# A row choice by repeated take-out of the eight largest, in the attention loop of a four-layer kernel

## The chip, the cores and the metric

One Trainium2 chip, one core. The time is the device time of one execution in microseconds (us). The engines are named as the profile names them: PE is the matrix engine (PEld is its loading of weights), DVE the vector engine, ACT the scalar engine, POOL the GpSimd engine, SP the one that issues DMAs.

## The reference

Four layers, each an attention part and a feed-forward part, on x (2 batches, 256 rows, 512 wide) and a context ctx (2 batches, 512 rows, 512 wide). Two parts matter here.

```python
# layer 2, attention: 32 query heads, 8 groups of keys and values, 128 wide
q, k = rmsnorm(q, q_norm_w), rmsnorm(repeat(k, 4), k_norm_w)
scores = einsum('bhqd,bhkd->bhqk', q, k) * scale + attention_mask      # 512 keys
out = einsum('bhqk,bhkd->bhqd', softmax(scores), v)
return out.transpose(...).reshape(B, Q, 32 * 128) @ o_proj_w.T

# layer 3, attention part: a choice among ctx's rows, for every batch and column
k = 154                                              # from 0.6 * 256, made even
_, topk_idx = top_k(moveaxis(ctx, 1, 2), k)          # largest 154 of 512, for each of 512 columns
mask = zeros(2, 512, 256).at[..., topk_idx].set(1.0) # indices of 256 and above drop out
crucial, subcrucial = mask * x, (1 - mask) * x       # then a small gate for each of the two
```

So before layer 3 can start, each of 2 x 512 columns of ctx needs the 154 largest of its 512 values marked, of which the first 256 places are used. This depends on ctx alone, so it can be worked out at any time before.

## The kernel before

ctx lies transposed in SBUF as `k.ctxT`, 128 partitions by 4 column blocks by 2 batches x 512 values. A "row tile" (`row_tile`, line 2280) is one block and batch: 128 partitions x 512 f32, eight of them (r = 0 to 7).

**The choice before.** A search by bits for each partition's 154th largest value. One round is four `bisection_count` calls (line 2320), each comparing two row tiles with the candidate bits and adding up the hits (L2324, 128x512), and one `bisection_update` of five tiny operations (L2374 to L2381, 128x8 and 128x16). Thirty-one rounds are spread over DVE's program: a start (eight counts at L2289, then L2297 to L2310) and the first counts in the layer-1 attention (one count call each at its units 40, 45, 50 and 55, an update behind the last), four counts in the layer-1 feed-forward part, four more and an update at the start of the layer-2 attention, and then two rounds in each of its steps. When the bits are found, `choose_piece` (line 2340) marks the chosen places, with the first ones first among equals, in five pieces for two row tiles: a count (L2347), equality (L2351) and the number left (L2352), a running sum (L2355), a comparison (L2358), an addition (L2362). Row tiles 0 and 1 are treated in units 4 to 7 of step 14, the other six in step 15.

**The layer-2 attention** (`layer2_attention`, line 1542) is 16 steps, one per group of heads and batch, numbered 0 to 15. Step 0 stands by itself, steps 1 to 14 are pairs in a hardware loop on PE, ACT and POOL; on DVE the loop holds steps 1 to 12, and 13 and 14 are written out. Step 15 is `run_final`. Every step has 8 units u (a head and 128 queries). In a unit, PE turns the probabilities (`turn_probs`, L1826), multiplies the scores of unit u + 2 (`scores`), and does a piece of other work: the projections of keys, values and queries of the next step (u = 0 to 4), the output projection of the step before (u = 5 to 7, `project_out`), the mix of probabilities and values (`mix`). ACT takes the exponentials (L1999) and casts the turned probabilities to their high part (L2007). DVE takes the low part (L2134, `probsT_low`), masks scores and takes their maximum (L2122, `maximum`), adds the output into x (L2140, `add_out`), and at the end of the unit runs two counts of the search. The order on each engine is the order of the code; engines meet by semaphores. There are two PSUM banks for scores (S) and two for turned probabilities (T), so PE's unit u + 2 needs DVE's maximum and ACT's exponential of unit u.

**Step 15** divides by the sum of exponentials ahead of the turn: DVE takes the reciprocal (L2181), scales the identity with it (L2183, `divided`), and PE multiplies by this diagonal (L1845, `turn_divided`). The mixed heads are split by ACT and DVE (`head_high`, `head_low`) and projected head by head (`project_final`, L1856). Two units of `project_out` for step 14 stand in it as well; they need POOL's scaling of step 14's heads (L1697, L1701, L1703), which in turn needs step 13's `add_out` of both halves. POOL also makes the low part of the weights in the loop (L1666, L1670, L1676; 2.4 to 4.6 us each).

## Time and profile before

| | us |
|---|---|
| median of 3 runs | 869.71 (868.5 to 871.69) |
| profiled execution | 867.53, with a span of 865.7 and 1.83 around it |
| busy in the span: PE / DVE / ACT / POOL | 779.5 / 716.7 / 517.8 / 416.6 |
| layer-2 attention, steps 1 to 14 | 273.7 to about 738.6 |
| layer-2 attention, step 15 | about 739 to 786 |

The times of single instructions come from one profiled execution. A row's microseconds are busy time; two instructions of an engine can overlap a little, so the distance from start to start says more about what an instruction takes. Idle time in brackets stands ahead of the row that ended it, with what released it. In a step a PE that is busy all the time sets the pace; a wait of PE is named with the engine that released it.

### The profile page before, as it was taken

To read this page: it belongs to the slowest core of one execution; us is meant where nothing else is said; L and a number is where in the kernel's file an instruction comes from. 1 tells how busy PE (TensorE), PEld (TensorE's weight loads), DVE (VectorE), ACT (ScalarE), POOL (GpSimd) and SP (SyncE) were. 2 spreads that over 40 slices of the span, in tenths; PEclk is the share of its full clock that TensorE was granted. 3 is DMA by queue.
4 is the path that set the end of the run, shared out by engine and by line. 5 is a ranking of instruction groups with operands and counts; after the bars stand their busy time and mean duration, and the time that the engine had idled before them with its cause. 6 is when DMAs were issued, how large, how long until landed. Compare 5 with 4: busy or idle time off the path is not lost. (4 is left out here: it accounts for less than half of the span.)

```text
span 865.7 us, 16485 instructions
## 1 busy us (share of the span) xinstructions
PE 779.5 (90%) x5172; PEld 633.8 (73%) x5178; DVE 716.7 (83%) x1751; ACT 517.8 (60%) x1407; POOL 416.6 (48%) x372
## 2 busy tenths in 40 slices
PE   1976899958987999999999999999999999689878
PEld 0474676534776898998898898898898898576356
DVE  7878998968787887887887887887887897894985
ACT  6865798836456756756656657657557557331521
POOL 3237078705236745745746746745744844501110
PEclk9999999979999999999999999999999999899989
DMA  8254246453202201201300300310220320003001
GB/s 308 92 170 149 75 149 217 157 167 108 68 32 59 88 26 52 94 24 45 101 24 26 119 25 22 109 39 14 86 71 0 97 73 0 25 1 119 1 1 48
DMA packets 38298, 66.65 MB, mean 77 GB/s; under 512 B 5553, under 2 KB 18417, under 8 KB 38130
## 3 DMA queue, kind: packets, MB, share of 16 engines
q1 hardware_dynamic: 38258, 66.15, 23.2%
q8 instruction: 21, 0.34, 0.2%
q14 instruction: 19, 0.16, 0.1%
HBM read 60.81 MB, written 5.34 MB: 76 GB/s over the span
## 5 line engine op out<-in xcount | busy, mean ns | idle before, releaser
L1999 ACT ACTIVATE layer_attention_probs<-xnT,stats 128x512 f32<-128x512 f32 x128 | 93.9, 734 | 134.1 <-DVE stats L2122 134.1
L2324 DVE TENSOR_SCALAR_CACHE_REDUCE xn<-ctxT,candidate 128x512 bf16<-128x512 f32 x240 | 168.7, 741 | 0.0
L1747 PE MATMUL bank<-layer_attention_keysT,layer_attention_queriesT 128*128 128x512 f32 x384 | 122.4, 427 | 5.0 <-DVE layer_attention_queriesT L2115 5.0
L2134 DVE TENSOR_TENSOR layer_attention_probsT<-bank,layer_attention_probsT 128x512 fp32r<-128x512 f32 x128 | 88.1, 688 | 42.2 <-ACT layer_attention_probsT L2007 40.8
L2007 ACT CAST layer_attention_probsT<-bank 128x512 fp32r<-128x512 f32 x128 | 74.9, 585 | 54.0 <-PE bank L1826 47.7
L1747 PEld LDWEIGHTS bank<-layer_attention_probsT,layer_attention_values 128*128 128x128 f32 x768 | 98.5, 188 | 11.7 <-DVE layer_attention_probsT L2134 6.5
L1747 PE MATMUL bank<-layer_attention_probsT,layer_attention_values 128*128 128x256 f32 x768 | 101.3, 281 | 3.4 <-DVE layer_attention_probsT L2134 3.0
L1747 PE MATMUL bank<-layer_attention_l_wq,layer_attention_xnT 128*128 128x512 f32 x384 | 93.7, 392 | 0.0
L1747 PEld LDWEIGHTS bank<-layer_attention_l_wkv,layer_context_parts 128*128 128x128 f32 x720 | 88.4, 188 | 2.8
L1747 PE MATMUL bank<-layer_attention_l_wkv,layer_context_parts 128*128 128x256 f32 x720 | 90.3, 278 | 0.0
L1747 PE MATMUL bank<-layer_attention_wo,layer_attention_headsT 128*128 128x512 f32 x336 | 88.8, 406 | 0.0
L2122 DVE CUSTOM_DVE_ANT_0 xnT<-bank,layer_attention_mask 128x512 f32<-128x512 f32 x128 | 87.0, 680 | 0.6 <-PE bank L1747 0.5
L1697 POOL TENSOR_TENSOR layer_attention_mixed<-layer_attention_mixed,xnT 128x512 f32<-128x512 f32 x30 | 49.1, 1636 | 68.9 <-DMA xnT<-inverse_sums 64.1
L1747 PEld LDWEIGHTS bank<-layer_attention_l_wq,layer_attention_xnT 128*128 128x128 f32 x384 | 70.9, 188 | 15.1 <-issue 0.2
L1826 PE MATMUL bank<-ident,layer_attention_probs 128*128 128x128 f32 x480 | 71.8, 272 | 0.4 <-ACT layer_attention_probs L1999 0.4
L1747 PEld LDWEIGHTS bank<-layer_attention_keysT,layer_attention_queriesT 128*128 128x128 f32 x384 | 63.4, 192 | 11.6 <-issue 5.8
L1747 PEld LDWEIGHTS bank<-layer_attention_wo,layer_attention_headsT 128*128 128x128 f32 x336 | 60.0, 189 | 11.5
L1826 PEld LDWEIGHTS bank<-ident,layer_attention_probs 128*128 128x128 f32 x480 | 57.5, 140 | 10.5 <-issue 0.6
L270 POOL TENSOR_TENSOR rstd<-varep,minus_half 128x1 f32<-128x1 f32 x24 | 14.9, 631 | 95.3 <-DVE varep L226 66.7
L1682 POOL TENSOR_SCALAR layer_attention_ssq<-layer_attention_ssq 128x4 f32<-128x4 f32 x48 | 9.3, 193 | 90.5 <-ACT layer_attention_squares L1958 90.5
L1958 ACT ACTIVATE layer_attention_squares<-bank 128x128 f32<-128x128 f32 x192 | 52.0, 299 | 0.0
L1687 POOL TENSOR_TENSOR xn<-xn,layer_attention_ssq 128x512 f32<-128x512 f32 x47 | 48.9, 1040 | 3.7
(332 smaller groups left out, 1716.1 us busy)
## 6 DMA issues: line engine op xcount, KB each, us to landing
layer_attention_l_raw_qo<-in_wqT SPq DMA_DIRECT2D x9, 1024.0 KB, 5.1
xnT<-inverse_sums SPq DMA_DIRECT2D x15, 512.0 KB, 3.7
layer_attention_l_raw_qo<-in_woT SPq DMA_DIRECT2D x7, 1024.0 KB, 6.9
tw_raw<-in_w_gateT SPq DMA_DIRECT2D x8, 688.0 KB, 5.5
tw_raw<-in_w_upT SPq DMA_DIRECT2D x8, 688.0 KB, 4.3
tw_raw<-in_w_downT SPq DMA_DIRECT2D x6, 768.0 KB, 4.6
layer_attention_l_raw_kv<-in_wkvT SPq DMA_DIRECT2D x9, 512.0 KB, 4.9
ternary<-tw_rounded SPq DMA_DIRECT2D x8, 344.0 KB, 2.5
```

The costliest lines, as they stand in the source:

```text
L270: g.tensor_tensor(k.rstd[:, t:t + 1], k.varep[:, t:t + 1], k.minus_half[:, 0:1], ALU.pow).then_inc(k.tile_rstd, 1)
L1682: own(g.tensor_scalar(ssq[:, c, :], ssq[:, c, :], 1.0 / HD, EPS, ALU.mult, ALU.add))
L1687: g.tensor_tensor(r, r, ssq[:, c, :].unsqueeze(2).broadcast_to([P, REP, HD]), ALU.mult)\
L1697: g.tensor_tensor(now, now, factors, ALU.mult).then_inc(S_["mix_scaled"], 1)
L1747: last = pe.matmul(out, stationary[f][a], moving[f][b], start=f == 0 and x == 0, stop=f == count - 1 and x == 2)
L1826: last = pe.transpose(T[u % 2][:, c * P:(c + 1) * P], probs[:, u % 3, c * P:(c + 1) * P], k.ident[:, :])
L1958: return a.activation(squares[:, h, :], source, ACT.Square, accum_out=ssq[:, c, h:h + 1])
L1999: a.activation(probs[:, u % 3, :], masked[:, u % 2, :], ACT.Exp, bias=negmax[:, u:u + 1], scale=-1.0, accum_out=sums[:, u:u + 1]).then_inc ...
L2007: a.copy(probsT[:, 0, p % 2, :, u % 2 * P:(u % 2 + 1) * P], T[u % 2][:, :].rearrange("p (c q) -> p c q", c=CPB)).then_inc(S_["probsT_high" ...
L2122: v.tensor_tensor_reduce(masked[:, u % 2, :], S[u % 2][:, :], mask[:, u % TPB, :], -1.0, 3.4e38, ALU.add, ALU.min, negmax[:, u:u + 1]).the ...
L2134: v.tensor_tensor(probsT[:, 1, p % 2, :, columns], T[u % 2][:, :].rearrange("p (c q) -> p c q", c=CPB), probsT[:, 0, p % 2, :, columns], A ...
L2324: own(k.nc.vector.tensor_scalar((k.flags if flags is None else flags)[:, r % 2], row_tile(k.ctxT, r), k.candidate[:, r:r + 1].bitcast(F32) ...
```

## The change

The search by bits goes, with its buffers, its flags and all its counts and updates. In its place each row tile's eight largest values are found (`largest`, the vector engine's max) and then taken out, that is, overwritten in place by the lowest f32 (`take_out`, match_replace), 20 times. 154 is 19 times 8 and 2, so ahead of the last take-out six of the eight values are set to the lowest f32 (`leave_rest`). What was overwritten is then turned into ones (`flag`, 128x256, the half that is used). A pass is 16 operations over 128x512 f32: one pass in step 0 (two operations a unit), 18 in steps 1 to 12 (three a unit), the last in step 13, the eight flags in step 14 (one a unit). Nothing of it is left in step 15, in the layer-1 parts, or ahead of step 0.

In step 15, DVE's division of unit u + 1 and ACT's exponential of unit u + 2 are issued in unit u. DVE's `probsT_low` follows the maximum in the same unit, and the two `add_out` come at u = 5 and 6. On PE `project_out` moves from u = 5, 6 to u = 4, 5, and three of the four `project_final` move ahead of the last mix.

```diff
+def largest(k, own, r):
+    own(k.nc.vector.max(k.top[:, r, :], row_tile(k.ctxT, r)))
+def take_out(k, own, r):
+    own(k.nc.vector.match_replace(row_tile(k.ctxT, r), k.top[:, r, :], row_tile(k.ctxT, r), GONE))
+def leave_rest(k, own):
+    own(k.nc.vector.memset(k.top[:, :, TOPK % TAKEN:TAKEN], GONE))
+def flag(k, own, r):
+    row = row_tile(k.ctxT, r)[:, 0:SEQ]
+    own(k.nc.vector.tensor_scalar(row, row, GONE, None, ALU.is_equal))
...
+    OPS = 2 * CTILES
+    ROUND = [(op, r) for half in range(2) for op in (largest, take_out) for r in range(half * CTILES // 2, (half + 1) * CTILES // 2)]
+    PER_BODY = 3
...
+                def search(step, u, own):
+                    if step[0] is not None:
+                        ops = (ROUND * PER_BODY)[(step[1] - 1) * PER_BODY * CTILES:step[1] * PER_BODY * CTILES]
+                    elif step[1] < STEPS - 2:
+                        ops = ROUND
+                    else:
+                        ops = [(flag, r) for r in range(CTILES)]
+                    now = ops[u * len(ops) // UNITS:(u + 1) * len(ops) // UNITS]
...
-                        if u < chosen_from:
-                            bisection_count(k, own, u % 4)
-                            if u % 4 == 3:
-                                bisection_update(k, own)
...
+                            search(step, u, own)
...
                 def run_final(step):                      # PE
...
+                        if u in (4, 5):
+                            for half in range(2):
+                                project_out(before, u - 4, half, weights=wq)
                         if u in (3, 5, 7):
                             mix(step, u // 2 - 1, final=True)
-                        if u in (5, 6):
-                            for half in range(2):
-                                project_out(before, u - 5, half, weights=wq)
-                    project_final(step, 0)
+                        if u in (6, 7):
+                            project_final(step, u - 6)
+                    project_final(step, 2)
                     mix(step, PAIRS - 1, final=True)
-                    for h in range(1, REP):
-                        project_final(step, h)
+                    project_final(step, 3)
...
                 def run_final(step):                      # DVE
+                    divided(step, 0)
+                    probsT_low(before, UNITS - 1)
+                    maximum(step, 1)
                     for u in range(UNITS):
-                        if u:
-                            probsT_low(step, u - 1)
-                        else:
-                            probsT_low(before, UNITS - 1)
-                        divided(step, u)
                         if u + 1 < UNITS:
-                            maximum(step, u + 1)
+                            divided(step, u + 1)
                         if u in (4, 6):
                             head_low(u // 2 - 2)
-                        if u == 7:
-                            add_out(before, 0)
-                        for r, piece in pieces[u * len(pieces) // UNITS:(u + 1) * len(pieces) // UNITS]:
-                            choose_piece(k, own, r, piece)
-                    probsT_low(step, UNITS - 1)
-                    add_out(before, 1)
+                        if u + 2 < UNITS:
+                            maximum(step, u + 2)
+                        probsT_low(step, u)
+                        if u in (5, 6):
+                            add_out(before, u - 5)
```

DVE in the loop, before, unit 7 of the first step of the pair and what follows it. Here L2324 is a count, L2374 to L2381 the update, L2140 the `add_out`, L2134 `probsT_low`; REGISTER_ALU rows only work out what a wait compares with.

```order
L2324 TENSOR_SCALAR xn,counts<-ctxT,candidate 128x512 x2
L132 REGISTER_ALU
L2374 SCALAR_TENSOR_TENSOR enough<-counts,flip 128x8
L132 REGISTER_ALU
L2376 TENSOR_TENSOR set_bit<-enough,bits 128x8
L132 REGISTER_ALU
L2378 TENSOR_TENSOR found<-found,set_bit 128x8
L2379 TENSOR_SCALAR bits<-bits 128x16
L132 REGISTER_ALU
L2381 TENSOR_TENSOR candidate<-found,bits 128x8
L2138 REGISTER_ALU
L2140 TENSOR_TENSOR x<-bank,x 128x512
```

The same place after the change. L2276 is a take-out, L2125 the `add_out`, L2119 `probsT_low`.

```order
L2123 REGISTER_ALU
L2125 TENSOR_TENSOR x<-bank,x 128x512
L132 REGISTER_ALU
L2276 MATCH_REPLACE ctxT<-top,ctxT 128x512 x3
L2123 REGISTER_ALU
L2125 TENSOR_TENSOR x<-bank,x 128x512
L2119 TENSOR_TENSOR layer_attention_probsT<-bank,layer_attention_probsT 128x4x128
L2103 REGISTER_ALU
```

Two counts and five tiny operations have become three take-outs; in units without an update, two counts have become three operations.

DVE where step 14 ends and step 15 begins, before. L2358 and L2362 are pieces of the choice, L2347 another; L2181 and L2183 the division, L2122 the maximum with its second row.

```order
L2140 TENSOR_TENSOR x<-bank,x 128x512
L2358 SCALAR_TENSOR_TENSOR ctxT<-ctxT,left 128x256 x2
L2362 TENSOR_TENSOR ctxT<-xn,ctxT 128x256 x2
L2140 TENSOR_TENSOR x<-bank,x 128x512
L2134 TENSOR_TENSOR layer_attention_probsT<-bank,layer_attention_probsT 128x4x128
L2181 RECIPROCAL layer_attention_last_inverse<-stats 128x1
L2183 TENSOR_SCALAR layer_attention_diagonal<-ident,layer_attention_last_inverse 128x128
L2122 ISA xnT,stats<-bank,layer_attention_mask 128x512
L2122 ISA stats 128x1
L2347 TENSOR_SCALAR xn,above<-ctxT,found 128x512 x2
L2134 TENSOR_TENSOR layer_attention_probsT<-bank,layer_attention_probsT 128x4x128
```

After the change, from the same `add_out` (L2125) on. L2287 is a flag, L2185 and L2187 the division, L2107 the maximum.

```order
L2125 TENSOR_TENSOR x<-bank,x 128x512
L2287 TENSOR_SCALAR ctxT<-ctxT 128x256
L2125 TENSOR_TENSOR x<-bank,x 128x512
L2185 RECIPROCAL layer_attention_last_inverse<-stats 128x1
L2187 TENSOR_SCALAR layer_attention_diagonal<-ident,layer_attention_last_inverse 128x128
L2119 TENSOR_TENSOR layer_attention_probsT<-bank,layer_attention_probsT 128x4x128
L2107 ISA xnT,stats<-bank,layer_attention_mask 128x512
L2107 ISA stats 128x1
L2185 RECIPROCAL layer_attention_last_inverse<-stats 128x1
L2187 TENSOR_SCALAR layer_attention_diagonal<-ident,layer_attention_last_inverse 128x128
L2107 ISA xnT,stats<-bank,layer_attention_mask 128x512
```

Four operations of the choice (x2 each for L2358 and L2362) are gone from ahead of the first division, one flag is in their place, and the division now stands ahead of `probsT_low` (L2119).

PE at the end of step 15, before. Products with headsT are `project_out`, with probsT and values a mix, L1856 `project_final`, L1845 a turn.

```order
L1747 MATMUL bank<-layer_attention_probsT,layer_attention_values 128x256 x12
L1747 MATMUL bank<-layer_attention_l_wq,layer_attention_headsT 128x512 x12
L1845 MATMUL bank<-layer_attention_diagonal,layer_attention_probs 128x128 x4
L1747 MATMUL bank<-layer_attention_l_wq,layer_attention_headsT 128x512 x12
L1845 MATMUL bank<-layer_attention_diagonal,layer_attention_probs 128x128 x4
L1747 MATMUL bank<-layer_attention_probsT,layer_attention_values 128x256 x12
L1856 MATMUL bank<-layer_attention_l_wq,layer_attention_xnT 128x512 x6
L1747 MATMUL bank<-layer_attention_probsT,layer_attention_values 128x256 x12
L1856 MATMUL bank<-layer_attention_l_wq,layer_attention_xnT 128x512 x18
```

After the change; L1839 is `project_final`, L1828 a turn.

```order
L1730 MATMUL bank<-layer_attention_l_wq,layer_attention_headsT 128x512 x12
L1730 MATMUL bank<-layer_attention_probsT,layer_attention_values 128x256 x12
L1828 MATMUL bank<-layer_attention_diagonal,layer_attention_probs 128x128 x4
L1839 MATMUL bank<-layer_attention_l_wq,layer_attention_xnT 128x512 x6
L1828 MATMUL bank<-layer_attention_diagonal,layer_attention_probs 128x128 x4
L1730 MATMUL bank<-layer_attention_probsT,layer_attention_values 128x256 x12
L1839 MATMUL bank<-layer_attention_l_wq,layer_attention_xnT 128x512 x12
L1730 MATMUL bank<-layer_attention_probsT,layer_attention_values 128x256 x12
L1839 MATMUL bank<-layer_attention_l_wq,layer_attention_xnT 128x512 x6
```

Six products of `project_final` now stand behind the turn of unit 6, twelve behind the mix of unit 7, and six instead of eighteen are left behind the last mix.

## Rows read from the trace of the kernel before

**Rows 1.** stretches (us): length; busy (count) of PE, PEld, DVE, ACT, POOL; clock; DMA
```profile
438.03:470.86 32.83, 32.83 (x216) 29.36 (x215) 26.49 (x76) 21.08 (x64) 16.12 (x16) 1.00 0.05 16
470.86:503.86 33.00, 32.86 (x214) 29.02 (x213) 29.08 (x75) 20.58 (x63) 23.08 (x18) 1.00 0.30 95
602.52:636.88 34.36, 32.85 (x214) 29.01 (x213) 30.46 (x76) 20.58 (x63) 23.14 (x18) 1.00 0.28 92
744.50:780.00 35.50, 28.22 (x164) 24.32 (x165) 31.14 (x83) 11.32 (x26) 5.62 (x5) 0.90 0.00 1
```

**Rows 2.** whom PE waited for, whole span: us, times, longest
```profile
PE bank L1845 <- DVE layer_attention_diagonal L2183: 11.9, 5, 5.2
PE bank L1747 <- DVE layer_attention_probsT L2134: 3.0, 4, 1.5
```

**Rows 3.** instructions in time (start, us, engine): counts in the loop
```profile
440.98 0.74 DVE L2324 TENSOR_SCALAR_CACHE_REDUCE xn<-ctxT,candidate 128x512 bf16<-128x512 f32 x1
441.64 0.74 DVE L2324 TENSOR_SCALAR_CACHE_REDUCE xn<-ctxT,candidate 128x512 bf16<-128x512 f32 x1
...
443.21 0.69 DVE L2140 TENSOR_TENSOR x<-bank,x 128x512 f32<-128x512 f32 x1
```

**Rows 4.** groups by line: busy us, mean ns; first operation of the update
```profile
L2374 DVE SCALAR_TENSOR_TENSOR enough<-counts,flip 128x8 f32<-128x8 f32 x31 | 24.7, 798 | 1.0
```

**Rows 5.** instructions in time, DVE in the router's choice after this layer
```profile
798.40 0.61 DVE L2605 MAX8 tail_best<-tail_expd 128x8 f32<-128x64 f32 x4 [0.48 <-ACT tail_expd L2765]
799.04 0.09 DVE L2608 MATCH_VALUE_LOAD tail_rest<-tail_best,tail_expd 128x8 f32 x1
...
799.25 0.08 DVE L2608 MATCH_VALUE_LOAD tail_rest<-tail_best,tail_expd 128x8 f32 x1
```

**Rows 6.** instructions in time, DVE, a reduction over 512 columns
```profile
86.39 1.89 DVE L1066 TENSOR_REDUCE layer_attention_negmax<-bank 128x1 f32<-128x512 f32 x3
```

**Rows 7.** instructions in time, DVE, POOL and PE, 608 to 611 us
```profile
608.08 1.52 DVE L2381 TENSOR_TENSOR candidate<-found,bits 128x8 int32<-128x8 int32 x1
607.99 1.58 POOL L1697 TENSOR_TENSOR layer_attention_mixed<-layer_attention_mixed,xnT 128x512 f32<-128x512 f32 x1 [0.46 <-DMA xnT<-inverse_sums]
610.85 1.67 PE L1747 MATMUL bank<-layer_attention_probsT,layer_attention_values 128*128 128x256 f32 x12 [1.51 <-DVE layer_attention_probsT L2134]
```

**Rows 8.** instructions in time, PE in the last step
```profile
738.97 0.96 PE L1747 MATMUL bank<-layer_attention_keysT,layer_attention_queriesT 128*128 128x512 f32 x3
745.17 2.04 PE L1845 MATMUL bank<-layer_attention_diagonal,layer_attention_probs 128*128 128x128 f32 x8 [5.24 <-DVE layer_attention_diagonal L2183]
...
749.65 1.05 PE L1845 MATMUL bank<-layer_attention_diagonal,layer_attention_probs 128*128 128x128 f32 x8
...
781.00 4.28 PE L1856 MATMUL bank<-layer_attention_l_wq,layer_attention_xnT 128*128 128x512 f32 x18
```

**Rows 9.** instructions in time, DVE and POOL in the last step
```profile
738.45 4.19 DVE L2358 SCALAR_TENSOR_TENSOR ctxT<-ctxT,left 128x256 f32<-128x256 f32 x2
753.49 1.14 DVE L2183 TENSOR_SCALAR layer_attention_diagonal<-ident,r_attention_last_inverse 128x128 f32<-128x128 f32 x1
736.01 4.60 POOL L1670 TENSOR_TENSOR layer_attention_l_wq<-layer_attention_l_raw_qo,layer_attention_l_wq 128x2048 fp32r<-128x2048 f32 x1 [3.51 <-ACT layer_attention_l_wq L2023]
740.84 1.52 POOL L1697 TENSOR_TENSOR layer_attention_mixed<-layer_attention_mixed,xnT 128x512 f32<-128x512 f32 x1 [0.23 <-DMA xnT<-inverse_sums]
753.28 1.26 POOL L1703 TENSOR_TENSOR layer_attention_headsT<-layer_attention_mixed,layer_attention_headsT 128x512 fp32r<-128x512 f32 x1
```

**Rows 10.** instructions in time, end of the layer-1 attention
```profile
170.20 0.69 ACT L1170 ACTIVATE layer_attention_probs<-bank,layer_attention_negmax 128x512 f32<-128x512 f32 x1 [2.61 <-DVE layer_attention_negmax L1066]
171.03 0.57 PE L964 MATMUL bank<-l_keysT,layer_attention_queriesT 128*128 128x512 f32 x1 [1.84 <-ACT layer_attention_probs L1170]
172.74 1.58 POOL L270 TENSOR_TENSOR rstd<-varep,minus_half 128x1 f32<-128x1 f32 x3
```

**Rows 11.** instructions in time, start of the layer-2 attention
```profile
247.15 0.93 PE L1747 MATMUL bank<-layer_attention_keysT,layer_attention_queriesT 128*128 128x512 f32 x3 [1.49 <-DVE layer_attention_queriesT L2115]
```

More of the change, by code:

```diff
@@ L1097, in latent_low @@
                      .then_inc(S_["latent_low"], 1)
-                k.flags = mixed[:, :].bitcast(BF16).rearrange("p (j c) -> p j c", j=2)
-                for j in range(4):
-                    bisection_start_count(k, own, j)
-                k.flags = k.xn[:, 3, :].bitcast(BF16).rearrange("p (j c) -> p j c", j=2)
                 value_copy(0)
@@ L2240, in _ @@
                 rowsT_low(start, KEYS)
-                for j in range(FRONT_COUNTS, 4):
-                    bisection_count(k, own, j, first_flags(k))
                 rowsT_low(start, 0)
```

156 lines of the change are left out of this document (33 added, 123 removed).

## The prediction

> **What bounds the kernel now.** I read the stretches first, one per step of the layer-2 attention. Steps without and with POOL's low parts take 32.83 and 33.00 us, and PE is busy for 32.83 and 32.86 of them at full clock [rows 1]. So the loop goes at PE's pace; DVE is busy 26.49 and 29.08 us, 27.8 in the mean. One step takes 34.36 us with the same work on PE. The next view, whom PE waited for, has only 3.0 us for `probsT_low` in the whole span, one wait being 1.5, but 11.9 us in five waits for the diagonal L2183 [rows 2]. That diagonal exists only in step 15, and there PE is busy 28.22 of 35.50 us at a clock of 0.90 [rows 1]. The instructions in time then tell who held DVE. Less search work on DVE is therefore worth nothing in most of the loop. The change is worth what it frees in step 15, and in the few places where an update or a count stands in front of something that PE needs.
>
> **The loop, steps 1 to 12.** A step has 16 counts. From start to start a count takes 0.66 to 0.67 us [rows 3], so 10.7 us go. Two updates go with them. The one at 442.31 takes 0.90 us up to `add_out` at 443.21 [rows 3]. But L2374 alone averages 798 ns over 31 updates [rows 4], many times what eight columns need, because it is often held up; I put an update at 1.5, two at 3.05. DVE's other work is then 27.8 − 10.7 − 3.05 = 14.1 us a step.
>
> Added are 24 operations a step, 12 maxima and 12 take-outs over 512 columns. The trace has both kinds only at 64 columns, in the router. Four maxima are busy 0.61 us together, the last for about 0.21, so they start 0.133 us apart; a load of the eight values and its replacement take 0.20 us (799.04 to 799.25) [rows 5]. For the 448 further columns I take the count's rate: it takes 0.67 us for 512, hardly anything being fixed, and three reductions over 512 columns are busy 1.89 us, 0.63 each [rows 6]. At 0.467 us for 448 columns a maximum takes 0.60 and a take-out 0.67. That is 12 x 0.60 + 12 x 0.67 = 15.2 us, and DVE comes to 29.3 of PE's 32.9 us, 89%. The bounds: below, nothing runs faster than the router's pieces, 0.133 and 0.20, which would leave DVE lighter than before at no gain, PE being full; above, a kind could run at half that rate, 0.93 us more than the 64-column price, 1.07 and 1.13. The lot may average (32.9 − 14.1) / 24 = 0.78 us until DVE sets the pace. I take 0.60 and 0.67, since both one-input rows over 512 columns lie there.
>
> PE hides all of that. What can be gained is PE's waits. In step 602.52 to 636.88, L2381 (128x8, two inputs) took 1.52 us beside POOL's L1697 of 1.58, and PE's mix at 610.85 waited 1.51 for the `probsT_low` behind it [rows 7]. The holds that I see fell on operations with two tensor inputs from SBUF, as here, or on the diagonal; the new operations have one, like the count, so I expect nothing of the choice to be held there: −1.5. Steps of 33.00 against 32.86 busy lose 0.14, six or seven times: −0.9. Against it, a unit without an update now has three operations instead of two, 1.9 to 2.0 us for 1.33. The slack for `probsT_low` there is small where another 0.14 us wait is already seen, so a few tenths a step may come back. I take nothing and keep up to 0.5 a step, 6 us, for the range.
>
> **Step 15.** PE goes from 739.75 (738.97 and a last score of step 14, busy 0.96, whose three products leave PE to step 15 after some 0.78) to 785.28 (781.00 + 4.28) [rows 8], 45.5 us. 11.9 are waits for the diagonal. The clock was 0.90 over 35.5 us, that is, its lower level for a fifth of them; a turn takes 2.04 us there and 1.05 at the full one [rows 8]. Half of 7 us would be 3.5, some of it inside waits; I take 3.1. Work is 45.5 − 11.9 − 3.1 = 30.5, 30.1 by the durations at full clock.
>
> The waits that come in their place:
> - The first turn waited 5.24 [rows 8], because L2358 held DVE (two, 4.19 us, from 738.45) with L2362 behind, beside POOL's L1670 (4.60 from 736.01) and L1697 (1.52 from 740.84) [rows 9]. Those pieces go, but POOL's do not. A flag, `add_out` and the division stand there now, and the diagonal took 1.14 us for 128 columns when it met L1703 [rows 9], where a count's rate would give under 0.3; a diagonal that meets L1697 ends only at 742.36. I put the first turn at 742.7, a wait of 2.95.
> - For units 2 and 3, maximum, exponential and division form a chain: two operations over 512 columns at 0.7 to 0.85 each [rows 3, 10] and 0.4 for reciprocal and diagonal, 2.0 to 2.2 us a unit, against a little less of PE's work: 1.2.
> - `project_out` now comes a unit earlier and `project_final` sits behind `add_out` of the same bank: 1.35. The last head's split before the last six products: 1.1.
>
> Together 6.6. The end is at 739.75 + 30.1 + 6.6 = 776.4, so 785.28 − 776.4 = 8.9, with the clock at full level because the longest stop is shorter; I take 9.1 with a small head start from step 14's shorter DVE program. Bounds: no wait at all gives 15; if each wait is only moved (POOL being the holder) 0 to 3.
>
> **The ends of the search elsewhere.** At the end of the layer-1 attention the last count and update stood ahead of the last maximum; ACT waited 2.61 for it and PE 1.84 behind [rows 10]. That goes, but POOL's rstd at 172.74 comes behind its own queue [rows 10] and holds the next normalization, so I take 1.6, between 0.5 and 3.2. At the start of the layer-2 attention four counts and an update go; PE's first scores waited 1.49 for the query rows [rows 11], which come 0.35 to 0.6 earlier: 0.6, at most 1.5. The counts at the very start and in the layer-1 feed-forward part stand where DVE waits for others anyway: nothing.
>
> **Sum.** 9.1 + 1.6 + 0.6 + 0.9 + 1.5 = 13.7. The profiled execution took 867.53, so 853.8. The median of the runs is 869.71, 2.2 above it: 856.0. With step 15's likely 6 to 13 and the small terms, this case alone spans 852 to 860.
>
> **Rivals.**
> - *The new operations set the pace (slower).* If the take-out costs 1.13 us, half rate, a step of DVE is 14.1 + 12 x 1.13 + 12 x 0.60 = 34.9 us, 2.0 above PE; twelve steps 24, plus waits that no longer pair up, 25: 856 + 25 = 881. It decides from a mean of 0.78. If both are slow, a step is 40.5 and the kernel about 950. For it: no 512-column row of either exists. Against it: the 64-column pair takes 0.20 us including a load, so that at half rate it would have only 0.07 fixed. Chance 0.10.
>  The Trainium skill, Vector Engine (DVE) Microarchitecture Reference, section "The match/index hardware and the swap-based sort pattern", describes the replacement as one preparing step and then one steady step over the stream, and the maximum as a chain of seventeen steps. By the first the take-out runs at one element a cycle, as the rival denies; the router's row of 0.20 us agrees, but no row here shows the 512-column case.
> - *The shorter slack gives it back.* 0.5 us a step in 12 steps, 6 us: 862. For it: DVE goes from 85 to 89% and each of 6 light units gets 0.6 us more. Against it: unit 7, the one with the updates and the stops, gets lighter. Chance 0.10.
> - *Step 15 stays held by POOL.* Divisions and flags meet L1697 and L1703 again, and only 3 of the 9 come: 862. For it: [rows 9]. Against it: the division now stands a unit ahead, so one hold is covered. Chance 0.07.
>  The Trainium skill, SBUF — State Buffer, section "SBUF: two separate sides", says that DVE and POOL share a port pair that one instruction holds to its end, wanted by DVE when it reads two inputs from SBUF or runs in a two-port mode. [Rows 7] (1.52 beside 1.58) agree. By it, the one-input maxima and take-outs pass POOL freely and only diagonals and flags are caught, which is this rival, with 3 us for 9.
> - *More than this*, PE without waits in step 15 and the layer-1 stop gone fully: 9 → 14 and 1.6 → 3, 849. Chance 0.08.
> The forecast has 0.65.
>
> 0.5% of the time, 4.35 us, is about what a measurement of this kernel tells from no change. Faster by more means below 865.4. The forecast, the last rival and nearly all of the two at 862 lie there, though their tails do not, and the first rival is slower: 0.82 faster, 0.08 the same, 0.10 slower. The range must leave out no more than a fifth: 850 to 866 leaves out the slow rival and half of the last.
>
> **What the profile of after would show.** MAX8 and the replacement over 128x512 near 0.68 us busy, 0.60 and 0.67 from start to start; a mean over 0.78 refutes the loop's term. PE busy about 32.8 of each step with DVE at 29.3 or so; a step of 33.4 is the second rival. No wait for `probsT_low` of 1.5 us. In step 15, waits for the diagonal of 6 us or less in all, the first of about 3, a clock of 0.95 or more; if the first is still 5, POOL was the holder. At the layer-1 end ACT's wait of 2.61 gone. The prediction is wrong above all if either new operation runs at half rate, since 288 of them stand in the loop.

## The result and the profile after

The changed kernel took 853.93 us in the median (853.17 to 858.18, 4 runs), the kernel before 870.32 (868.5 to 871.69), a ratio of 0.983 (0.981 to 0.985). Forecast were 856.0 and a range of 850 to 866. The profiled execution has a span of 851.5 us against 865.7, which is 14.2 less; the medians lie 16.4 apart.

First the stretches of the changed kernel (called after from here on): two steps of the loop that follow each other, one earlier step that differs, and step 15. Columns as in [rows 1].

```profile
432.60:465.40 32.80, 32.80 (x214) 29.38 (x213) 29.06 (x69) 21.30 (x64) 16.11 (x16) 1.00 0.05 16
465.40:498.20 32.80, 32.80 (x215) 29.39 (x214) 29.24 (x69) 20.77 (x63) 23.13 (x18) 1.00 0.29 96
337.31:370.94 33.63, 33.09 (x214) 29.46 (x213) 28.91 (x69) 20.57 (x63) 19.34 (x18) 1.00 0.28 95
729.50:771.30 41.80, 34.69 (x204) 29.38 (x203) 23.24 (x53) 13.10 (x30) 10.22 (x7) 0.96 0.04 14
```

Where [rows 1] had 32.83 and 33.00 us, the loop's ordinary steps now take 32.80. PE is busy in all of it, and DVE is busy 29.06 and 29.24. One step still takes 33.63, where PE waited 0.54 us for the values' low parts. In step 15 the granted clock is 0.96, and DVE is busy 23.24 of 41.80 us, where it was busy 31.14 of 35.50.

The two new operations, by their line: count, shortest, median and longest duration in ns, first and last start. Then places in time where several stand in a row:

```profile
L2276 DVE MATCH_VALUE_LOAD ctxT<-top,ctxT x160: 70/82/89, 248.4 to 694.8; 128x8 f32 x160
L2276 DVE MATCH_REPLACE8 ctxT<-top,ctxT x160: 670/676/681, 248.5 to 694.9; 128x512 f32<-128x512 f32 x160
```

```profile
L2271 DVE MAX8 top<-ctxT x160: 673/681/693, 242.6 to 680.9; 128x8 f32<-128x512 f32 x160
```

```profile
501.65 0.67 DVE L2276 MATCH_REPLACE8 ctxT<-top,ctxT 128x512 f32<-128x512 f32 x1
...
502.31 0.68 DVE L2276 MATCH_REPLACE8 ctxT<-top,ctxT 128x512 f32<-128x512 f32 x1
...
504.70 1.87 DVE L2271 MAX8 top<-ctxT 128x8 f32<-128x512 f32 x3
```

Both run at one rate: three maxima are busy 1.87 us, so they start 0.60 apart ((1.87 − 0.68) / 2), and two take-outs start 0.66 apart (501.65 to 502.31), load included. Forecast were 0.60 and 0.67. None of the 320 is stretched: the longest took 693 ns, though POOL was at work beside some two thirds of them, and 115 of them began while a POOL operation of over 1.2 us still had 0.15 us or more to go.

Whom PE waited for, of which [rows 2] had 11.9 and 3.0 us:

```profile
PE bank L1828 <- DVE layer_attention_diagonal L2187: 3.6, 3, 2.5
...
PE bank L1839 <- DVE x L2125: 1.3, 1, 1.3
...
PE bank L1839 <- DVE layer_attention_xnT L2192: 0.9, 1, 0.9
```

The wait for `probsT_low` in the loop is gone. In step 15 PE waits 3.6 + 1.3 + 0.9 = 5.8 us, where the forecast had 6.6. The rows in time, to be read against [rows 8, 9], show where the longest of these waits comes from:

```profile
728.21 4.60 POOL L1653 TENSOR_TENSOR layer_attention_l_wq<-layer_attention_l_raw_qo,layer_attention_l_wq 128x2048 fp32r<-128x2048 f32 x1 [3.51 <-ACT layer_attention_l_wq L2007]
732.92 1.51 POOL L1680 TENSOR_TENSOR layer_attention_mixed<-layer_attention_mixed,xnT 128x512 f32<-128x512 f32 x1
```

```profile
730.65 2.31 DVE L2287 TENSOR_SCALAR ctxT<-ctxT 128x256 f32<-128x256 f32 x1
732.89 0.68 DVE L2125 TENSOR_TENSOR x<-bank,x 128x512 f32<-128x512 f32 x1
...
733.67 0.85 DVE L2187 TENSOR_SCALAR layer_attention_diagonal<-ident,r_attention_last_inverse 128x128 f32<-128x128 f32 x1
```

```profile
734.66 2.05 PE L1828 MATMUL bank<-layer_attention_diagonal,layer_attention_probs 128*128 128x128 f32 x8 [2.55 <-DVE layer_attention_diagonal L2187]
```

The flag that now stands where L2358 stood is held for 2.31 us, up to the end of POOL's 4.60 (732.81); six of the eight flags take 0.28 to 0.39. The diagonal behind it takes 0.85 us and ends about when POOL's 1.51 does (734.52 and 734.43). The turn starts 2.55 us late.

**Where the gain sits.** One profiled execution is one sample, and the twelve experiments below share most of the kernel, so each stretch has up to thirteen samples of after's code and one of before's. In this table a stretch runs from an instruction to an instruction: the first reduction L1064 of the layer-1 attention (L1066 in before), the first turn of layer_ffn_x, the first, ninth, 113th and 121st maximum of the layer-2 attention, PE's first product behind it, and the end of DVE's last addition. "Same code" is the mean over all traces of kernels whose code in the stretch is that of after, with their number and the lowest and highest.

| stretch | before | after | same code as after |
|---|---|---|---|
| start to layer-1 attention | 86.4 | 86.2 | 88.0 (13; 85.8 to 91.8) |
| layer-1 attention | 100.7 | 96.3 | 97.2 (11; 96.3 to 97.8) |
| layer-1 feed-forward, start of layer 2 | 57.9 | 56.3 | 57.9 (13; 56.3 to 58.9) |
| step 0 | 30.3 | 31.5 | 30.9 (13; 30.4 to 33.0) |
| steps 1 to 13 | 429.1 | 426.5 | 426.8 (8; 425.4 to 427.5) |
| step 14 | 32.8 | 32.7 | 32.7 (13; 32.7 to 32.7) |
| step 15 | 49.4 | 41.9 | 41.9 (9; 40.7 to 42.4) |
| behind it | 76.6 | 77.6 | 77.8 (13; 75.8 to 79.1) |

Three stretches are shorter than before by more than the same code scatters: the layer-1 attention by 3.4 us, steps 1 to 13 by 2.4, step 15 by 7.5, together 13.3. In the other stretches before lies within the same code's scatter or 0.1 us beside it, although the feed-forward part, the start of layer 2 and step 0 lost counts too; the very start alone spans 6 us. The trace pair's own difference, 14.2, is larger than 13.3 by chance: after's trace is shorter than the same-code mean by 1.6 us in the feed-forward part and by 0.9 in the layer-1 attention, while its step 0 and what lies behind step 15 took 1.2 and 1.0 more than before's.

The 13.3 us are not all of the difference between the medians, which differ by 16.4 here and by 15.6 in a second session. Before was traced once, in an execution 2.8 us below its median, so the runs don't show where the other 2 to 3 us lie.

### The profile page after: what moved, and what is told of

It reads as the page before. It is cut to its first block and busy times, and to the rows that moved or that the text cites. A ratio compares the mean times of both kernels' runs of the same rounds, so it can differ in the third digit from the quotient of the medians.

```text
span 851.5 us, 16269 instructions
## 1 busy us (share of the span) xinstructions
PE 777.6 (91%) x5178; PEld 637.2 (75%) x5178; DVE 681.0 (80%) x1512; ACT 520.2 (61%) x1407; POOL 416.0 (49%) x372
## 5 line engine op out<-in xcount | busy, mean ns | idle before, releaser
L1730 PE MATMUL bank<-layer_attention_keysT,layer_attention_queriesT 128*128 128x512 f32 x384 | 120.6, 422 | 4.2 <-DVE layer_attention_queriesT L2100 4.1
L2119 DVE TENSOR_TENSOR layer_attention_probsT<-bank,layer_attention_probsT 128x512 fp32r<-128x512 f32 x128 | 87.4, 683 | 44.0 <-ACT layer_attention_probsT L1991 43.0
L2276 DVE MATCH_REPLACE8 ctxT<-top,ctxT 128x512 f32<-128x512 f32 x160 | 106.9, 676 | 0.0
L2271 DVE MAX8 top<-ctxT 128x8 f32<-128x512 f32 x160 | 102.4, 681 | 0.0
L1730 PE MATMUL bank<-layer_attention_l_wkv,layer_context_parts 128*128 128x256 f32 x720 | 92.9, 281 | 0.0
L1730 PEld LDWEIGHTS bank<-layer_attention_l_wkv,layer_context_parts 128*128 128x128 f32 x720 | 90.7, 188 | 2.5
L2107 DVE CUSTOM_DVE_ANT_0 xnT<-bank,layer_attention_mask 128x512 f32<-128x512 f32 x128 | 87.1, 680 | 5.3 <-PE bank L1730 5.1
L1064 DVE TENSOR_REDUCE layer_attention_negmax<-bank 128x1 f32<-128x512 f32 x64 | 43.4, 685 | 9.4 <-PE bank L962 8.7
```

The lines of the kernel that those rows point to most:

```text
L1064: v.tensor_reduce(negmax[:, tile(u), head(u):head(u) + 1], S[u % 3][:, :], AX.X, ALU.max, negate=True)\
L1730: last = pe.matmul(out, stationary[f][a], moving[f][b], start=f == 0 and x == 0, stop=f == count - 1 and x == 2)
L2107: v.tensor_tensor_reduce(masked[:, u % 2, :], S[u % 2][:, :], mask[:, u % TPB, :], -1.0, 3.4e38, ALU.add, ALU.min, negmax[:, u:u + 1]).the ...
L2119: v.tensor_tensor(probsT[:, 1, p % 2, :, columns], T[u % 2][:, :].rearrange("p (c q) -> p c q", c=CPB), probsT[:, 0, p % 2, :, columns], A ...
L2271: own(k.nc.vector.max(k.top[:, r, :], row_tile(k.ctxT, r)))
L2276: own(k.nc.vector.match_replace(row_tile(k.ctxT, r), k.top[:, r, :], row_tile(k.ctxT, r), GONE))
```

## The experiments

Each is an edit of the changed kernel, timed beside runs of the kernel before on the same chip. Since the start of the kernel scatters by 6 us with no edit, a median tells differences of some 4 us only; the verdicts on smaller ones rest on the stretch that the edit touches, with the table's same-code scatter as the measure. Each of these stretches was traced once for each kernel.

### The changed kernel again

> The changed kernel once more, as the base for its neighbours on this chip. 853 to 855 us, ratio 0.983 to the kernel before. If the two-microsecond scatter of its tail (a TensorE clock that falls around 811 us in the earlier trace) is chance, the part behind the layer-2 attention may differ by up to 1 us from the earlier trace.

857.04 us (852.69 to 858.89), ratio 0.9825 (0.979 to 0.986). The expected 853 to 855 was missed, but the ratio holds: the median moved 3 us with the session, and that of the kernel before 2. Its trace has 78.1 us behind step 15, which is less than 1 us from after's 77.6, as expected, and a step 15 of 40.7. That step ran at a granted clock of 1.00, where after's ran at 0.96. In the nine traces of step 15's unchanged code there are two at 1.00, with 40.7 and 40.9 us, and seven at 0.96, with 41.9 to 42.4, 42.2 in the mean. The small differences below are therefore also read against the mean at the same clock.

### Step 15 with the old order

```diff
 def run_final(step):                      # DVE; PE and ACT likewise as before
-    divided(step, 0)
-    probsT_low(before, UNITS - 1)
-    maximum(step, 1)
     for u in range(UNITS):
+        probsT_low(step, u - 1) if u else probsT_low(before, UNITS - 1)
-        if u + 1 < UNITS: divided(step, u + 1)
+        divided(step, u)
...
```

> The changed kernel with the old order of step 15 on PE, ACT and DVE; the choice pieces stay gone. It splits the 7.5 us that the traces show for step 15 into the pieces' removal and the new order. My expectation: the pieces carry more than half; without the look-ahead each unit's division waits for its exponential again and the end has three head products after the last split: 3 us given back, 857. Rival A (the order carries it): 860 to 861. Rival B (the pieces carry all): 854.

858.52 us, ratio 0.985 (0.982 to 0.988), and step 15 takes 42.8 us (same code 41.9). By this the order is worth 0.9 us of the 7.5, and 0.6 if only traces at this kernel's clock of 0.96 are compared; the removed pieces are worth the remaining 6.6; they were not put back by themselves. That is rival B but for a microsecond, and my 3 us was too much. PE's waits show what the order does:

```profile
PE bank L1828 <- DVE layer_attention_diagonal L2185: 6.6, 4, 2.7
```

With the old order PE waits 6.6 us for diagonals, 3.0 more than in after, but none for `add_out` or for a head's split (1.3 + 0.9 in after). The new order has 3.0 us less of waits for the diagonal and pays for them with 2.2 us of waits at the end.

### What holds the first turn: flags later, diagonals on ACT, both

```diff
-                        ops = [(flag, r) for r in range(CTILES)]
+                        ops = [(flag, r) for r in range(CTILES - 2)]   # late_flags: one a unit, u = 0 to 5
...
+                        if u in (3, 4):                                # late_flags, step 15
+                            flag(k, own, CTILES - 2 + u - 3)
```

```diff
-                    v.wait_ge(S_["last_inverted"], u + 1)              # act_diag: gone from DVE
-                    v.tensor_scalar(diagonal[:, u % 2, :], k.ident[:, :], last_inverse[:, u:u + 1], None, ALU.mult)
+                    a.wait_ge(S_["last_inverted"], u + 1)              # act_diag: on ACT, u + 1 in unit u
+                    a.activation(diagonal[:, u % 2, :], k.ident[:, :], ACT.Copy, scale=last_inverse[:, u:u + 1])
```

> The last two of the eight flags move from step 14 behind the maxima of units 3 and 4 of step 15. Theory (the flag held by POOL sets the first turn): the first wait for the diagonal falls from 2.55 to about 1.2, since the diagonal itself then waits for POOL's 4.6 us operation that ends near 732.8 and for the next; 852.7 us. Rival (POOL is the holder, whatever stands first): 2.5 us stays, 854.

> ACT instead of DVE scales the identity in step 15; all else as changed. Theory (DVE and POOL hold each other for operations on the identity): the diagonal no longer takes 0.85, 0.82 and 0.45 us in units 0, 2, 3, and the waits of 0.72 and 0.31 us go; the first wait stays near 2.0 because the flag in front of the reciprocal is still held 2.3 us. 852.7 us, 1.2 less. Rival (the waits are the chain of maximum, exponential and division, whoever does the last): 854, no change.

> Both edits together: nothing of DVE's that POOL can hold stands between the last exponential of step 14 and the first turns of step 15. Theory: the first wait falls to 0.3 or less, units 2 and 3 have none, the clock stays at its upper level there: 3.6 us of waits and some 1 us of slow turns go, 850 us. Rival (the turns then wait for the scores' maxima instead, the chain through DVE and ACT): 852.5 us.

| | median us | ratio to before | step 15 us | clock there | PE's waits for the diagonal |
|---|---|---|---|---|---|
| changed kernel, same session | 857.04 | 0.9825 (0.979 to 0.986) | 40.7 (same code 41.9) | 1.00 | 2.7, 0.7, 0.3 |
| flags later | 852.11 | 0.9765 (0.973 to 0.980) | 39.1 | 1.00 | 0.9, 1.0, 0.3 |
| diagonals on ACT | 855.96 | 0.9818 (0.978 to 0.986) | 41.3 | 0.96 | 0.3, 0.4; 2.1 for `probsT_low` |
| both | 854.22 | 0.9789 (0.975 to 0.983) | 38.0 | 1.00 | 0.4, 0.3, 0.4 |

Rows in time of the flags-later kernel around its first turn, PE, DVE and POOL:

```profile
733.58 4.60 POOL L1653 TENSOR_TENSOR layer_attention_l_wq<-layer_attention_l_raw_qo,layer_attention_l_wq 128x2048 fp32r<-128x2048 f32 x1 [3.52 <-ACT layer_attention_l_wq L2007]
...
737.18 1.09 DVE L2187 TENSOR_SCALAR layer_attention_diagonal<-ident,r_attention_last_inverse 128x128 f32<-128x128 f32 x1
...
738.41 1.13 PE L1828 MATMUL bank<-layer_attention_diagonal,layer_attention_probs 128*128 128x128 f32 x8 [0.93 <-DVE layer_attention_diagonal L2187]
...
742.39 1.58 POOL L1680 TENSOR_TENSOR layer_attention_mixed<-layer_attention_mixed,xnT 128x512 f32<-128x512 f32 x1
...
742.99 1.07 DVE L2187 TENSOR_SCALAR layer_attention_diagonal<-ident,r_attention_last_inverse 128x128 f32<-128x128 f32 x1
...
744.21 1.13 PE L1828 MATMUL bank<-layer_attention_diagonal,layer_attention_probs 128*128 128x128 f32 x8 [0.97 <-DVE layer_attention_diagonal L2187]
```

With the flag away the diagonal itself meets the same POOL operation: it ends at 738.2, when POOL's 4.60 us from 733.58 do. Unit 2's takes 1.07 us beside POOL's 1.58. So POOL's operation is what the diagonal waits out both times, and the flag only made it longer. ACT's scaling is not held, as the kernel with both edits shows; the last row is the stretch of its step 15, columns as in [rows 1]:

```profile
731.64 4.62 POOL L1653 TENSOR_TENSOR layer_attention_l_wq<-layer_attention_l_raw_qo,layer_attention_l_wq 128x2048 fp32r<-128x2048 f32 x1 [3.52 <-ACT layer_attention_l_wq L2007]
...
735.35 0.40 ACT L2019 ACTIVATE layer_attention_diagonal<-ident,r_attention_last_inverse 128x128 f32<-128x128 f32 x1
...
735.90 1.13 PE L1828 MATMUL bank<-layer_attention_diagonal,layer_attention_probs 128*128 128x128 f32 x8 [0.38 <-ACT layer_attention_diagonal L2019]
...
740.48 0.40 ACT L2019 ACTIVATE layer_attention_diagonal<-ident,r_attention_last_inverse 128x128 f32<-128x128 f32 x1 [0.23 <-DVE r_attention_last_inverse L2195]
740.48 1.52 POOL L1680 TENSOR_TENSOR layer_attention_mixed<-layer_attention_mixed,xnT 128x512 f32<-128x512 f32 x1
...
741.02 1.13 PE L1828 MATMUL bank<-layer_attention_diagonal,layer_attention_probs 128*128 128x128 f32 x8 [0.31 <-ACT layer_attention_diagonal L2019]
...
732.86:770.87 38.01, 33.38 (x204) 28.20 (x203) 18.36 (x46) 15.91 (x38) 10.33 (x7) 1.00 0.05 15
```

Both of ACT's take 0.40 us with POOL at work beside them, and the first turn waits 0.38. Step 15 is at 38.0 us, 3.9 under the same-code mean and 2.7 under the lowest of the nine. PE's waits for diagonals fell from 3.6 us to 1.1; 3.6 of waits and 1 of slow turns were expected to go. Against the two same-code traces that ran at 1.00 too, with 40.8 us in the mean, the gain is 2.8 us, which is what the waits explain (3.8 and 3.9 us in those two, 1.1 here). The rest of the 3.9 is the clock, and that the edits brought it to 1.00 isn't shown, since the unedited code reached it with a first wait of 2.7 us. Each edit alone brought less: the later flags 2.7 us, 1.7 at the same clock; the diagonals on ACT 0.6, 0.9 at the same clock, since the flag still stood in front and PE's first turn then waited 2.1 us for `probsT_low`. Whether these kernels beat the changed one in the median can't be told, as the intervals overlap.

### The layer-1 calls put back

```diff
+                    if u in (40, 45, 50, 55):                          # l1_last: only 55
+                        own.wait()
+                        for r in range(2 if u < 55 else 4):
+                            largest(k, own, r)
```

> The changed kernel with a stand-in for the last count call and update in the layer-1 attention: four maxima over 512 columns, 2.4 us of DVE against 2.66 before, at unit 55. The prediction counted 1.6 us for this place, because POOL's rstd behind was thought to hold the rows: by it 855.5. By the two traces' starts the place is worth 3.5 us up to the next scores' product and some 1.6 us more at the lower clock: 857.5 to 859.

> As l1_last, with two maxima each at units 40, 45 and 50 as well. By the prediction, which counted the earlier calls at nothing, 855.5; by the traces, where PE stood 1.4 us earlier at the corresponding place ahead of the last call, 1.4 us more than l1_last: 859 to 860.4.

858.19 us, ratio 0.9855 (0.983 to 0.989), and 861.37, 0.987 (0.984 to 0.991). The stretch of the layer-1 attention in four kernels, before, after, last call, all calls:

```profile
86.40:187.10 100.70, 86.14 (x900) 61.25 (x901) 87.80 (x173) 79.03 (x198) 54.60 (x43) 0.96 0.42 139
```

```profile
86.20:182.50 96.30, 83.30 (x900) 60.14 (x901) 80.53 (x143) 78.95 (x198) 54.78 (x43) 0.96 0.44 145
```

```profile
87.60:186.30 98.70, 83.75 (x899) 59.66 (x899) 83.71 (x147) 78.93 (x198) 55.07 (x43) 0.97 0.42 141
```

```profile
89.50:190.30 100.80, 85.18 (x900) 60.89 (x901) 87.08 (x154) 79.14 (x198) 55.04 (x43) 0.94 0.41 138
```

Four calls bring 100.8 us, where before had 100.7; the last call alone brings 98.7 against 97.2. That makes the last call and its update worth 1.5, as the prediction had it, and not the 3.5 and more that I read from the two traces; the three calls ahead of it, counted at nothing, are worth the other 1.9. That the calls together carry the whole 3.4 us is clear of the same code's scatter of 96.3 to 97.8. How they share it is less certain: each share rests on one trace, and 98.7 lies only 1.0 above that scatter.

### The loop without the choice, and with more of it

```diff
-                        ops = (ROUND * PER_BODY)[...]        # no_take
+                        ops = []
...
                     for op, r in now:
                         op(k, own, r)
+                    if step[0] is not None and u in (0, 2, 4, 6):      # loop_28; loop_32: every u
+                        own(v.max(k.spare[:, u % 3, :], mask[:, 0, :]))
```

> Steps 1 to 12 without any maximum or take-out; the other passes stay. Leaves out 18 of the 20 passes of the row choice. Theory (PE sets the loop's pace and hides DVE's 29 of 32.8 us): 0.3 to 1 us less, 853.2. Rival (the tight units still cost a few tenths a step): 3 to 6 us less, 848 to 851.

> One more maximum over 512 columns in units 0, 2, 4 and 6 of steps 1 to 12: 28 operations a step, DVE 29.15 + 4 x 0.61 = 31.6 of PE's 32.8 us. Theory (only the sum against PE's step matters): 0 to 2 us more, 855. Rival (a single unit that is too full passes its delay to PE, which never makes it up): 0.3 to 0.5 a unit held, 5 us or more, 859 to 865.

> One more maximum in each unit of steps 1 to 12: 32 operations a step, 29.15 + 8 x 0.61 = 34.0 us against 32.8. Theory (from a mean of (32.9 - 14.1) / 24 on, DVE sets the pace): at least 12 x 1.2 = 15 us more, 869, and more where DVE also waits for ACT and PE, up to 885. Rival (DVE's busy time is overstated by overlapping records, about 0.07 us an instruction, 69 a step): it still fits, 856 to 860.

Medians 858.17 (0.986, 0.983 to 0.989), 857.1 (0.984, 0.980 to 0.987) and 868.24 (0.994, 0.991 to 0.997). The stretch of steps 1 to 13 of after, then of the kernels with none, 28 and 32 operations a step:

```profile
270.30:696.80 426.50, 425.66 (x2747) 381.12 (x2748) 373.82 (x877) 272.76 (x818) 256.11 (x222) 1.00 0.18 59
```

```profile
274.10:700.70 426.60, 425.29 (x2747) 381.06 (x2748) 199.57 (x445) 270.92 (x818) 256.66 (x222) 1.00 0.18 59
```

```profile
272.50:699.90 427.40, 426.22 (x2747) 380.55 (x2748) 399.51 (x925) 272.49 (x818) 258.73 (x222) 1.00 0.18 59
```

```profile
279.20:715.10 435.90, 430.65 (x2747) 379.76 (x2748) 423.74 (x972) 271.17 (x818) 256.81 (x222) 1.00 0.18 58
```

Between 199.57 and 399.51 us of DVE's busy time nothing happens to the length: 426.6 without any of it, 426.8 with 24 operations a step, 427.4 with 28. At 32 it is 435.9, 9.1 more, 0.76 for each of the twelve steps. DVE then has hardly a gap between its instructions, 5.8 us in the twelve steps together, where after's DVE has 45.9. Its step is 32.8 + 0.76 = 33.6 us, 4.8 of them the eight maxima at 0.60, so that the changed kernel's DVE work is at most 28.8 from start to start. The first theory holds: PE hides the choice up to its own pace. My 15 us for 32 operations used busy time, which overstates by the overlaps, and the median of 868.24 came near my 869 by luck: the kernel with 28 operations was already at 857.1 in that session, and I had counted from 854. That taking 18 passes out makes the loop no faster shows that none of the second rival's price was paid.

Two cautions. First, the 32 operations have one maximum at the end of unit 7 that the 28 don't have, and the next section shows that place to be tight by itself; how much of the 9.1 us is its share wasn't tested. Second, PE can lose time without a gap in its row: at 32 its busy time is 430.65 us for 425.66 with the same products at the same clock, so 5.0 of the 9.1 us stand inside the busy time of PE. A step in which PE is busy all the time is thus not yet one in which it waits for nothing; the length of the step tells.

### Five tiny operations at the end of unit 7

```diff
+                    if step[0] is not None and u == 7:
+                        for _ in range(5):
+                            own.wait()
+                            own(v.tensor_tensor(k.spare[:, 0, :], k.spare[:, 1, :], k.spare[:, 2, :], ALU.mult))   # tiny_two
+                            # tiny_one: own(v.tensor_reduce(k.spare[:, 0, 0:1], k.spare[:, 1, :], AX.X, ALU.max))
```

> Five tiny operations (128x8) with two tensor inputs from SBUF, each waiting for the one before, at the end of unit 7 of steps 1 to 12, as the old update had at its end. Theory (such an operation is held while POOL works): about 0.2 us each when free, up to 1.5 or 2.3 when POOL is in the middle of one of its own, a mean of 0.4 to 0.5, and one or two waits of PE for probsT_low of about 1.5 us: 856. Rival (the old stall was the update's length, not its inputs): 0.17 us each, no change, 854.

> The same with one tensor input (a maximum over 8 columns into one). Theory of the held input pair: every one of the 60 takes its 0.1 to 0.2 us whatever POOL does, and the time is that of the changed kernel, 854. Rival (POOL slows any small DVE operation on SBUF): long ones among them as in tiny_two.

869.38 us (0.996, 0.994 to 0.999) and 864.79 (0.993, 0.989 to 0.996). Steps 1 to 13 take 440.6 and 434.9 us against 426.8: 13.8 and 8.1 more. Both are far above what I expected, and for two reasons that the rows let one tell apart. First the added line of the two-input kernel and of the one-input kernel, with shortest, median and longest in ns; then one held group of five with POOL's operation beside it and the stretch behind PE's stop (columns as in [rows 1]), and one of the other kernel that POOL's also reaches into; last PE's waits in the two:

```profile
L2145 DVE TENSOR_TENSOR spare<-spare x60: 166/166/1547, 309.2 to 683.9; 128x8 f32<-128x8 f32 x60
```

```profile
L2145 DVE TENSOR_REDUCE spare<-spare x60: 160/161/165, 311.1 to 680.6; 128x1 f32<-128x8 f32 x60
```

```profile
376.11 2.35 DVE L2145 TENSOR_TENSOR spare<-spare 128x8 f32<-128x8 f32 x5
...
376.68 1.56 POOL L1682 TENSOR_TENSOR layer_attention_mixed<-layer_attention_mixed,xnT 128x512 f32<-128x512 f32 x1 [9.05 <-DMA xnT<-inverse_sums]
...
379.80:383.60 3.80, 3.77 (x19) 3.80 (x20) 3.80 (x9) 1.94 (x5) 2.00 (x3) 0.55 0.00 0
```

```profile
445.38 0.94 DVE L2145 TENSOR_REDUCE spare<-spare 128x1 f32<-128x8 f32 x5
...
446.00 1.60 POOL L1682 TENSOR_TENSOR layer_attention_mixed<-layer_attention_mixed,xnT 128x512 f32<-128x512 f32 x1 [9.12 <-DMA xnT<-inverse_sums]
```

```profile
PE bank L1732 <- DVE layer_attention_probsT L2121: 8.2, 12, 1.8
```

```profile
PE bank L1732 <- DVE layer_attention_probsT L2121: 4.0, 12, 0.4
```

With two inputs from SBUF the longest operation took 1547 ns for a median of 166, and three of twelve groups took 2.24 to 2.35 us, each with a POOL operation that began inside it; with one input no operation took over 165 ns and no group over 0.95 us. That is the hold, as expected: exactly three of the sixty operations with two inputs began while a long POOL operation had 0.15 us or more to go, and all three were held. The comparison is a weak one on the other side: POOL's operations begin later in the one-input groups and overlap them by 0.33 us at most, so only two of those sixty began while one had 0.15 us or more to go, and the two kernels' operations differ in kind too, a product against a maximum. The stronger evidence for one input is the 115 maxima and take-outs that began beside POOL and took no longer than the rest. The three held groups are 1.3 to 1.4 us longer than the others. Two of their steps are longer by as much; the third is longer by 3.0, and there PE's granted clock was 0.55 for 3.8 us behind the stop of 1.8, so that 1.6 us of slow products come on top of the hold.

The other part is a surprise. Even the operations that nothing held, 0.9 us a step, cost 0.67 us a step, and PE waited for `probsT_low` in all twelve, for 4.0 us of the 8.1; another 3.7 stand inside its busy time again (429.3 us against after's 425.7). So the border between unit 7 and unit 0 had only 0.2 us left in the changed kernel (a group delays the next operation by 0.89, from 512.28 to 513.17, and 0.67 of it arrives at PE), though DVE is idle for 4 of a step's 32.8 us. `loop_28` put 2.4 us into a step, in units 0, 2, 4 and 6, and paid next to nothing.

## Why the prediction was right, step by step

- **PE sets the loop's pace and hides the choice.** Right, and shown by the kernel without it (426.6 against 426.8) and by the room that is left: 28 operations fit, 32 don't. By the prediction the mean of 24 operations may reach 0.78 us; with a room of 32.8 − 28.8 = 4.0 us it comes to 0.80, if the room can be used anywhere.
- **0.60 and 0.67 us for the new operations.** Measured 0.60 and 0.66. The fixed part from the 64-column rows and the rate from neighbours with one input gave both. The slow rival (881) had its condition refuted.
- **Loop: −1.5 for a hold that can't happen any more, −0.9 for small waits.** 2.4 forecast, 2.4 measured. That two inputs from SBUF meet the hold is what the tiny operations show, and that one input doesn't is what the 320 new operations show. The Trainium skill, SBUF — State Buffer, section "SBUF: two separate sides", gives that rule; the traces agree (with two inputs up to 1547 ns for a usual 166, with one 693 at most for a usual 676 to 681). It also names the two-port modes. Flags and diagonals have one tensor input and were held too (2.31, 1.09 us), which fits if they run in such a mode: a free flag takes 0.28 us for 256 columns, where other operations over 256 columns take 0.42. That they do run in it isn't shown.
- **The second rival, the slack gives it back (862).** It didn't, but a place with only 0.2 us of slack was near. The prediction put "a few tenths" on a unit with three operations for two; the tight place turned out to be the end of unit 7, which had become lighter by the update that left. Operations as long as the update's 0.9 us beside the three take-outs bring 8 us back.
- **Step 15: −9.1.** Measured −7.5, inside 6 to 13. The wait terms were 6.6 and came to 5.8, with the first at 2.55 for 2.95. What was mis-sized is the rest: 45.5 − 7.5 = 38.0 us less 5.8 of waits leaves 32.2 of PE's work, where I had 30.1. The prediction took all of the slow clock's 3.1 us as gained, "because the longest stop is shorter". But the trace of after has 0.96, not 1.00, with a first turn of 2.05 us. PE was busy 34.69 us in the stretch, and 33.36 in an execution of the same kernel that stayed at the upper level:

```profile
729.70:770.35 40.65, 33.36 (x205) 28.16 (x204) 23.31 (x53) 13.00 (x30) 10.20 (x7) 1.00 0.04 14
```

  So 1.3 of the 3.1 us stayed; the other 0.8 is work that I had counted too short. The reason given for the clock was wrong too: the two executions at 1.00 had first waits of 2.7 and 2.9 us, longer than after's 2.55.
- **The share of the two causes there** was not forecast apart, and when I put a number on it before the run it was wrong: 0.9 us for the order, not 3. Nearly all of the stretch's gain comes from the choice's pieces having left it; the rewritten order trades waits for waits.
- **Layer-1 attention: −1.6.** Measured −3.4; the step that failed is the one that counted only the last call. With the last call alone put back, 1.5 us return, and with the other three 1.9 more, as far as one trace each tells. The argument that POOL's rstd would hold the next normalization was wrong too: in after it starts at 169.22 instead of 172.74, still right behind POOL's own queue, which had moved forward with everything else.
- **Start of layer 2: −0.6.** Not seen: the stretch is 57.9 before and 57.9 in the mean after, with a standard deviation of 0.65. Up to a microsecond stays open.
- **The sum** was 13.7 and the three stretches give 13.3, but this closeness is partly luck: the errors +1.8 in layer 1 and −1.6 in step 15 nearly cancel. The median fell by 16.4, 2.7 more than forecast, and 2 to 3 us of it don't show in the traces.

## What to carry to other kernels

An engine that doesn't set the pace can take on a whole algorithm for free, and the test is a threshold, not a share: here DVE went from 0 to 28 operations a step with less than a microsecond's change in twelve steps, and at 32 it had hardly a gap left and the steps became longer. But the room is not the idle sum; it is the smallest slack in front of one operation that the pace-setting engine needs next, 0.2 us here against 4 us idle. In the last, unlooped step look for what another engine can hold in front of the first result, and move it away or to an engine that isn't held: here that was worth 2.8 us at the same clock, where rewriting the order was worth less than 1.

## What the runs showed of the hardware

- The same instructions up to the layer-1 attention took between 85.8 and 91.8 us in thirteen executions. The granted clock from 45 to 85 us goes with it for the most part: 0.96 in six executions of 85.8 to 87.6 us, 0.91 in four of 87.6 to 89.5, 0.87 in the two of 90.7 and 91.8; but one took 89.1 us at 0.96. The rows are of after and of the slowest:

```profile
45.00:85.00 40.00, 28.97 (x186) 24.54 (x187) 26.05 (x41) 23.39 (x38) 21.96 (x14) 0.96 0.51 172
```

```profile
45.00:85.00 40.00, 30.51 (x187) 26.27 (x186) 24.32 (x37) 22.30 (x35) 17.30 (x12) 0.87 0.47 150
```

- Step 15 of the same code took 40.7 and 40.9 us at a granted clock of 1.00, and 41.9 to 42.4 at 0.96, where slow products follow PE's stop (the first turn took 2.05 us in after, and 1.13 in the two at 1.00). The length of the stop doesn't decide it: 2.7 and 2.9 us at 1.00, 2.55 to 2.9 at 0.96. What decides isn't shown.
- Five operations over eight columns, each waiting for the one before, cost 0.94 us together, more than one maximum over 512 columns at 0.60.
